# A mixture of experts: the overflow tiles' weights move from GpSimd's row-wise gather to plain transfers on SyncE, addressed through a register

## What is computed

```python
logits = x @ gate_w.T
topv, topi = jax.lax.top_k(logits, TOP_K)                  # TOP_K = 8, E = 64
rw = jax.nn.softmax(topv.astype(jnp.float32), axis=-1).astype(x.dtype)
W = jnp.zeros((N, E), x.dtype).at[jnp.arange(N)[:, None], topi].set(rw)
gu = jnp.einsum('nh,eih->nei', x, gu_w)
gate, up = (gu[..., :I], gu[..., I:])                      # I = 128
inter_w = jax.nn.silu(gate) * up * W[:, :, None]
out = jnp.einsum('nei,ehi->nh', inter_w, dp_w)             # plus a shared expert
```

## Time and profile before

| | |
|---|---|
| median of 3 runs | 3014.05 us (3012.68 to 3017.73) |
| profiled execution | 3016.01 us |
| its span, first to last instruction | 3014.1 us |
| mean granted TensorE clock | 0.969 |
| PE / DVE / ACT / POOL busy | 93% / 50% / 32% / 23% |
| second mixture's tile loop | about 2465 to 2932 us |

### The profile page before, as it was taken

The page is one execution under the profiler, slowest core; times in us unless marked ns, Lnnn a source line. Parts: engine busy times, 40 slices in busy tenths (PEclk is TensorE's granted clock), DMA queues, the critical chain, the costliest instruction groups (busy, mean ns, idle before and its releaser), DMA issues.

```text
span 3014.1 us, 37838 instructions
## 1 busy us (share of the span) xinstructions
PE 2809.8 (93%) x14808; PEld 1777.9 (59%) x14808; DVE 1517.1 (50%) x2855; ACT 978.0 (32%) x2540; POOL 683.2 (23%) x676
## 2 busy tenths in 40 slices
PE   8999989998999999999998999999988988878888
PEld 4555555555756656687554555555555656666666
DVE  4545655766555566311467667665477661111115
ACT  2320341204443333221462322332144433333331
POOL 0150113500200000242023222110000226656640
PEclk9999999999799999999999999999999989999999
DMA  4110121100011011585000011011001037754447
GB/s 175 42 56 21 57 99 42 46 9 1 33 67 36 28 39 46 200 318 171 24 32 15 13 36 37 27 46 43 21 29 53 33 95 247 251 188 155 142 150 185
DMA packets 66677, 249.12 MB, mean 83 GB/s; under 512 B 26554, under 2 KB 28602, under 8 KB 53764
## 3 DMA queue, kind: packets, MB, share of 16 engines
q1 hardware_dynamic: 31776, 177.88, 17.5%
q0 software_dynamic: 31344, 65.30, 6.6%
q10 hardware_dynamic: 3380, 3.53, 0.4%
HBM read 274.53 MB, written 42.13 MB: 105 GB/s over the span
## 4 chain that ended last, share of the span: by engine, by line
PE 74%; DVE 13%; ACT 5%; another core or an unknown queue 3%; issue 2%; DMA 2%; POOL 1%; SPq 0%; ACTq 0%; POOLq 0%; DVEq 0%
PE P L1089 19%; PE P L1556 10%; PE P L1093 10%; PE P L1206 5%; PE P L1442 4%; PE P L1099 4%; PE P L1424 4%; PE P L1164 2%; PE P L1165 2%; PE P L1101 1%; PE P L1118 1%; ACT A L1722 1%; PE P L1415 1%; DVE A L2350 1%
## 5 line engine op out<-in xcount | busy, mean ns | idle before, releaser
L1616 ACT ACTIVATE A<-P 128x400 f32<-128x400 f32 (+4 forms) x589 | 302.2, 530 | 566.3 <-PE P L1442 170.9
L2626 DVE TENSOR_TENSOR A<-P,A 128x128 f32<-128x128 f32 (+1 forms) x141 | 44.9, 318 | 554.7 <-ACT A L1905 492.1
L1089 PE MATMUL P<-A,W 128*128 128x400 f32 x840 | 312.4, 509 | 5.4 <-DVE A L2274 2.9
L1089 PE MATMUL P<-X,W 128*128 128x400 f32 x816 | 305.0, 511 | 11.6 <-DMA W<-weights 8.8
L1089 PEld LDWEIGHTS P<-A,W 128*128 128x128 f32 x840 | 159.6, 193 | 126.4 <-issue 9.0
L1089 PEld LDWEIGHTS P<-X,W 128*128 128x128 f32 x816 | 154.7, 193 | 129.6 <-issue 16.2
L1099 PE MATMUL P<-C,A 128*128 128x128 f32 (+5 forms) x1463 | 205.3, 263 | 15.2 <-DVE A L2240 6.4
L1099 PEld LDWEIGHTS P<-C,A 128*128 128x128 f32 (+5 forms) x1463 | 166.9, 145 | 62.5 <-issue 44.5
L2757 POOL DMA_INDIRECT A<-tokens,A x141 | 144.5, 1025 | 195.5 <-issue 76.9
L1816 ACT ACTIVATE A<-P,small 100x361 f32<-100x361 f32 x256 | 142.6, 561 | 140.7 <-DVE small L2359 140.7
L1556 PE MATMUL P<-A 128*128 128x128 f32 x1280 | 159.2, 283 | 23.9 <-ACT A L1616 22.0
(11 more groups left out here) (378 smaller groups left out, 5089.6 us busy)
## 6 DMA issues: line engine op xcount, KB each, us to landing
W<-weights SPq DMA_DIRECT2D x60, 1024.0 KB, 4.8
A<-experts SPq DMA_DIRECT2D x16, 1536.0 KB
W<-experts SPq DMA_DIRECT2D x28, 768.0 KB
KT<-experts SPq DMA_DIRECT2D x15, 768.0 KB
W<-weights SPq DMA_DIRECT2D x17, 640.0 KB, 3.9
A<-experts SPq DMA_DIRECT2D x14, 768.0 KB
A<-outputs SPq DMA_DIRECT2D x12, 768.0 KB
W<-outputs SPq DMA_DIRECT2D x8, 768.0 KB
```

The source lines that it names most:

```text
L1089: self.e.matmul(out, a, b, start=i == 0, stop=False)
L1616: self.e.activation(out, in_, ACT.Copy).then_inc(*self.of(*item))
```

## The change

In the second mixture POOL no longer issues the further tiles' weights. SP walks the whole of `c.seq` in order. For a further tile it waits as before for the place to be free, then for `rows`, loads the tile's first row number (`WI[0, d]`, lane 0) from SBUF into a register, and issues one plain transfer of 128 consecutive rows from that row on. The transfer carries a condition: if the row number isn't below 128 * E, the whole transfer is skipped and its semaphore is still counted up. `first & 128 * (E - 1)` keeps the address inside the table in that case. The semaphore is that of the place, `expert{i % 9}`, as for an expert's own weights. In the first mixture nothing changes.

```diff
     def fetch_w(self, c, i):
         n, (d, expert) = c.n, c.seq[i]
-        if expert is None:
+        if expert is None and n == 5:
             self.wait_ge(self.at("rows", n))
             self.wait_ge(self.at("proj", "edown", n, i - c.R))
             self.rows(c.places()[i % c.R][0], None, c.table, c.WI[:, d:d + 1], 128 * c.E - 1, "got_w", n, i)
...
         for i, (d, expert) in enumerate(c.seq):
-            if expert is None:
+            place, needs = c.places()[i % R]
+            if expert is None and c.n == 5:
                 continue
-            place, needs = c.places()[i % R]
             for item in needs if i < R else [("proj", "edown", c.n, i - R)]:
                 self.wait_ge(self.at(*item))
-            self.dma(f"expert{i % R}", place, c.table[128 * expert:128 * expert + 128, :], "got_w", c.n, i)
+            if expert is None:
+                self.wait_ge(self.at("rows", c.n))
+                first = self.e.value_load(c.WI[0:1, d:d + 1], min_val=0, max_val=2 ** 17)
+                self.further(c, i, place, first)
+            else:
+                self.dma(f"expert{i % R}", place, c.table[128 * expert:128 * expert + 128, :], "got_w", c.n, i)
...
+    def further(self, c, i, place, first):
+        lane = f"expert{i % c.R}"
+        n = self.issued[lane] = self.issued[lane] + 1
+        sem = self.k.semaphore(lane)
+        self.e.dma_start(place, c.table[bass.ds(first & 128 * (c.E - 1), 128), :], cond=first < 128 * c.E).then_inc(sem, 16)
+        self.k.note(("got_w", c.n, i), Event(sem, 16 * n, lane, n))
```

More of the change, by code:

```diff
@@ L275, in op, with value_load @@
         return self
+    def value_load(self, *args, **kw):
+        return 0
     matmul = transpose = activation = tensor_copy = tensor_tensor = tensor_scalar = scalar_tensor_tensor = op
```

## The result

The changed kernel takes 2941.78 us (median of 4 runs, 2940.38 to 2945.13) beside 3013.36 for the kernel before (4 runs, 3008.70 to 3017.73): ratio 0.9762, 95% interval 0.9747 to 0.9776, 72 us less. The prediction was 2939 with 2912 to 2994. The profiled execution took 2940.38 (before: 3016.01), 75.6 less; the sum of the prediction said 75.

A forecast was written before the change was run, and what follows sets the result against it. POOL's software issuing, 1.67 us each, was taken to bound the second mixture's loop. 94 tiles x (4.22 - 3.42) = 75 us off 3016 gives 2941 profiled, 2939 us median; forecast's own range 2916 to 2975, 8 in 10 range 2912 to 2994.

The forecast's parts named there:

- the sum of the prediction: Second mixture's loop: 94 tiles, each going from 4.22 to 3.42 us, save 75 us.
- The limit: Second mixture's loop: POOL's issuing, or the queue behind it, sets the pace; 2.5 issues a tile at 1.67 us make 4.2.
- The size: Second mixture's loop: a tile falls from 4.22 to 3.42 us, the middle of 3.34 and 3.51; bounds 3.18 and 3.8.
- the excess of 1.04: Second mixture's loop: time per tile above PE's own 3.18 us, 98 us over 94 tiles.
- The register load: On SP, for each of 49 further tiles: reading a row number from SBUF takes 1 us, between 0.03 and 4.8.
- The cover of seven tiles: On SP: weights are issued seven steps, 24 us, before use, so even 5.5 us is hidden; otherwise 49 us in all.
- The DMA rival: Loop's first half: DMA engines no busier than 77 to 79% hold a tile at 3.89 us, total 2961; chance 0.16.
- The rival of another cause: Second mixture: POOL's issues were hidden and the stalls come from elsewhere; 3014, or 3005 with a lighter queue; chance 0.11.
- The jumps: Second mixture: single late starts of ScalarE's step, such as 4.34 us idle where 1.19 is ordinary, making up the excess.
- What would show it: Signs in the new profile: 49 fewer POOL issues, tiles 3.2 to 3.5 us apart, unknown queue under 30 us, higher clock.
- the unknown queue: Chain of waits from 2485 to 2911 us: 82 us, 19.3%, with no named cause, expected to fall under 30.
- SP's paired issues: On SP: a further tile's transfer and the plain one beside it, expected with gaps of 1 to 2 us.

The follow-up runs named there:

- experiment 9: Changed kernel with three register loads added on SP before the used one for each further tile: 2949.40 us, ratio 0.9782 to the kernel before.
- the first group of experiments: Four variants of the kernel before or the changed kernel, run on one chip where the kernel before takes 2919.12 us: 2916.18 to 2919.65 us.

## Why the prediction was right

**The limit.** The step that carried the forecast was to read 1.67 us per issue as a cost of POOL's issuing or of the queue behind it, though the record of one shows 1.0 and POOL is busy for 60% of the loop. The experiments show that it was right as a price per issue; which of the two places the time is lost in, they don't show. 116 to 123 issues pass in 200 us in kernels with two, two and a half and three issues a tile, with 10.6 to 29.3 MB in the software queue, and the tile takes what its issues take (1.68 us is 200 us over 119 issues):

| kernel | issues a tile | x 1.68 us | tile measured, us | total, us |
|---|---|---|---|---|
| every second fetch left out | 1.5 | 2.52 (PE's 3.18 holds) | 3.17 | 2919.2 |
| changed | 2 | 3.36 | 3.39 | 2940.6 |
| changed, 49 idle issues | 2.5 | 4.20 | 4.08 | 3017.4 |
| before | 2.5 | 4.20 | 4.26 | 3016.5 |
| changed, 98 idle issues | 3 | 5.04 | 5.00 | 3099.4 |

(A tile measured is 200 us over the count of L1913 or L1916 in the window from 2485, so one tile more or less in the count moves it by 0.05 to 0.12; that of before is the earlier trace rows's.)

**The size.** 3.42 us a tile was taken from between 3.34 and 3.51; 3.39 was measured. 4.22 - 3.39 = 0.83 over 94 tiles is 78 us; the profiled executions differ by 75.6. Against 2939 the median is 3 us higher, because the changed kernel's profiled execution was 1.4 us under its median, where that of before was 2.7 us over. One bound was misdescribed: 3.8 us a tile keeps 0.62 of the excess of 1.04, not half of it, which would be 3.70. Nothing else hangs on it.

**The register load.** 1 us was taken for the register load, between 0.03 and 4.8; from the load's start to the transfer's it is 0.9, the arithmetic included. The Trainium skill (DMA: Bandwidth & Descriptors, Latency and other measured facts) gives about 600 ns as the floor of a register load. The trace has 268 to 902 ns with a median of 277, below that floor; here the source is a number in SBUF, and the measurement decides. The cover of seven tiles held for 0.9 us and for nearly all of the 2.3 us that experiment 9 added.

**The DMA rival.** The share was expected at 90% and is 81%: the 200 us hold 59 tiles with 0.94 MB each (55.3 MB in all queues) where 47 had 1.01, since the window now reaches further past the last tile that a token needs. When all 49 are moved the share is 90%, and the time is 2.2 us longer, within the noise. At 3.39 us a tile this rival is out.

**The rival of another cause.** The jumps do come from POOL's issues, whatever carries the delay to ScalarE. The rule of the Trainium skill that spoke for it (DMA: Bandwidth & Descriptors, Issuing engines are not separate DMA queues), that another issuer saves only the issuing and that this is usually little, is right in its first half: moving the bytes to the other queue saved nothing, since 49 issues without bytes took all of the gain back. In its second half it doesn't fit a loop in which issuing is what's scarce: 49 issues fewer were 72 us, 1.5 us each.

**What would show it.** 49 fewer issues on POOL, tiles at 3.39 in both halves, the unknown queue from 82 us to none, the clock from 0.94 to 1.00, no jump of 4 us: all as written. SP's paired issues mostly stand 2.2 us apart, a little over the 1 to 2 that were named.

**What wasn't seen.** That the price of 1.67 us is not everywhere the same. On the chip of the first group of experiments a software issue took 1.32 us, the kernel before (with 20 semaphores) had no jumps at all, and by the time of the kernel before, 2919 us, the change would have had next to nothing to win. Nothing in a profile of one chip could tell that; the 2916 us of PE alone lie inside the range because 3.18 a tile was one of its bounds, not because such a chip was thought of. That the change was timed where an issue costs 1.67 us is the luck in this forecast's success; it was made from a profile with that price in it, and it holds for that price.

**What stays open** is what fills the gap between 1.32 and 1.68 us. It isn't the indices (16 do as badly as 128), the bytes, the twelve semaphores, the DMA engines' share or the granted clock. ScalarE and POOL both have idle times that end with "remote", so the trace names no releaser. The kernel's code narrows it a little. ScalarE's L1905 waits only for PE's up-projection of its tile and for VectorE's product (L2626) of two tiles before. In the earlier trace rows the former ends at 2568.2, as far as the trace models its end, and the latter is long done, yet L1905 starts at 2571.27, 3.0 us later. So in that jump ScalarE isn't waiting for a transfer to land; what keeps it is not shown.

## What to carry to other kernels

Count the instructions of a queue per unit of work and per microsecond in several windows: a rate that stays the same while bytes, tiles and waits change is a limit, even if the engine's busy share is only 60%. An indirect transfer that found nothing to move cost as much issuing as a full one here (1.00 us on its record, 119 issues in 200 us with both), so the weights of whole tiles were better moved as plain transfers by an engine that is idle, with the address and the condition in a register (0.9 us of SP from load to transfer, and mostly 0.12 us or less for the issue of a skipped one). Before trusting a gain that hangs on such a rate, run both kernels on more than one chip.

## What the hardware showed beyond that

Chips differ. The same kernel before takes 2919 us on one and 3013 to 3017 on others. Nearly all of it lies in this loop: with 20 semaphores the two profiled executions differ by 101.7 us, of which 2.7 are there when the loop begins (L2600 at 2463.1 and 2465.8) and 101.8 when its last tile is done (L1913 at 2831.4 and 2933.2). A software issue can be had every 1.32 us on the one and every 1.63 to 1.72 on the others, while PE's tile is 3.17 to 3.18 us on both. An instruction's record of 1.02 us is the same on both, too: the difference is in gaps, mostly of 1 to 3 us, between runs of issues that stand 1.32 apart. In the trace some of them end with "remote", some with "issue" and some with ScalarE's copy of a result, which is itself late. Each chip was used in one group of runs only, so a difference between chips isn't told from one between occasions.

DMA engines at a share of 90% over 200 us (311 GB/s) delayed nothing that the loop waited for at 3.39 us a tile.
